# Two gelu layers of an MLP: bank products copied to SBUF, gelu on two tiles at a time

## The reference

```
h = silu(lin(x, w1_w, w1_s)) * lin(x, w2_w, w2_s)
h = gelu(lin(h, h1_w, h1_s), approximate=False)
h = gelu(lin(h, h2_w, h2_s), approximate=False)
return lin(h, w3_w, w3_s)
```

## Time and profile before

| | us |
|---|---|
| median of 3 runs (lowest, highest) | 5497.53 (5493.53, 5498.82) |
| the profiled execution's own time | 5515.07 |
| its span in the trace | 5513.2 |
| granted clock of TensorE, mean over the span | 0.876 |
| PE, DVE, ACT, POOL busy | 4705.2, 3863.6, 3379.4, 3919.7 |
| ACT table loads: L1337, L1343, L1266 | 64, 64, 112 |

### The profile page before, as it was taken

How to read it: one execution, slowest core, us unless ns; L and a number is a source line. 1 busy time by engine, 2 the same in 40 slices (tenths; PEclk the granted TensorE clock), 3 DMA queues, 4 the chain that set the end, 5 groups by cost and what they waited for, 6 DMA issues and landing times. The chain is left out here.

```text
span 5513.2 us, 68556 instructions
## 1 busy us (share of the span) xinstructions
PE 4705.2 (85%) x21152; PEld 1806.6 (33%) x21152; DVE 3863.6 (70%) x4244; ACT 3379.4 (61%) x3966; POOL 3919.7 (71%) x2272
## 2 busy tenths in 40 slices
PE   8649998998999899898989998998999795199991
PEld 4301112223223222222232232222222344188880
DVE  6758888888988898889889888988898502100003
ACT  5646666778776877777777778777777532011111
POOL 0059998998999899899989998998899300411114
PEclk9855558989999999999989999999999896599995
DMA  3357666776777677766767776776677221255542
GB/s 104 107 199 255 239 232 222 266 259 234 247 253 249 224 257 259 251 234 241 265 235 248 259 258 228 256 258 251 233 251 252 101 84 50 102 178 177 178 166 95
DMA packets 313969, 1166.11 MB, mean 212 GB/s; under 512 B 70672, under 2 KB 120336, under 8 KB 303632
## 3 DMA queue, kind: packets, MB, share of 16 engines
q1 hardware_dynamic: 295088, 1058.96, 55.0%
q0 software_dynamic: 18528, 102.77, 5.6%
HBM read 1106.28 MB, written 65.80 MB: 213 GB/s over the span
## 5 line engine op out<-in xcount | busy, mean ns | idle before, releaser
L1609 POOL TENSOR_TENSOR s_h<-s_decay,s_h 128x768 f32<-128x768 f32 x2048 | 3708.0, 1850 | 272.8 <-ACT s_decay L1261 247.2
L1647 DVE TENSOR_TENSOR s_h<-s_h,bank 128x1024 f32<-128x1024 f32 x2048 | 2470.5, 1216 | 389.7 <-POOL s_h L1609 210.6
L1261 ACT ACTIVATE s_decay<-s_decay,s_a_neg 128x1536 f32<-128x1536 f32 x1024 | 1605.8, 1568 | 127.7 <-DMA s_decay<-dt_rows 127.0
L893 PE MATMUL bank<-s_h,s_cdiag 128*32 128x512 f32 x8192 | 1251.7, 687 | 5.8 <-ACT s_y L1273 5.8
L1266 ACT ACTIVATE bank<-bank,s_a_neg 128x512 f32<-128x512 f32 x1024 | 672.7, 657 | 735.5 <-PE bank L881 732.4
L867 PE MATMUL bank<-s_vrow,s_brow 9*128 9x512 bf16 x4096 | 844.8, 422 | 266.6 <-DVE s_h L1647 238.9
L1637 DVE TENSOR_TENSOR s_h<-bank,s_h 128x512 f32<-128x512 f32 x1024 | 699.5, 683 | 0.2
L867 PEld LDWEIGHTS bank<-s_vrow,s_brow 9*128 9x128 bf16 x4096 | 208.6, 92 | 1488.6 <-issue 1485.2
L1005 PE MATMUL bank<-m_mb,m_w 128*128 128x512 f32 x1024 | 524.8, 642 | 0.9 <-ACT m_mb L1339 0.9
L991 PE MATMUL bank<-m_ma,m_w 128*128 128x512 f32 x1024 | 519.2, 636 | 0.0
L881 PE MATMUL bank<-s_drow,s_unit 3*128 3x512 bf16 x1024 | 433.1, 423 | 75.7 <-DMA s_drow<-dt_parts 46.6
(11 more groups left out here) (200 smaller groups left out, 3898.0 us busy)
## 6 DMA issues: line engine op xcount, KB each, us to landing
s_decay<-dt_rows SPq DMA_DIRECT2D x1024, 768.0 KB, 5.4
m_w<-in_units SPq DMA_DIRECT2D x210, 512.0 KB, 5.2
s_vrow<-v_parts SPq DMA_DIRECT2D x1024, 36.0 KB
s_brow<-b_parts SPq DMA_DIRECT2D x1024, 9.0 KB
v_parts<-p_part SPq DMA_DIRECT2D x24, 512.0 KB, 3.0
slots<-in_x_tiles SPq DMA_DIRECT2D x128, 80.0 KB, 4.7
e_xs<-slots SPq DMA_DIRECT2D x39, 256.0 KB
expert_out<-e_made SPq DMA_DIRECT2D x39, 256.0 KB, 5.7
```

Of the source, the lines that this page charges most:

```text
L893: mm = pe.matmul(bank[q * 32:(q + 1) * 32, Y0], cdiag[:, hf * LANES + q, at * BLK:(at + 1) * BLK], h[:, t % 2, hf * LANES + q], start=(at ...
L1261: act.activation(decay[:, k % RING], decay[:, k % RING], ACT.Exp, scale=a_neg[:, 1:2]).then_inc(decay_ok, 1)
L1609: pool.tensor_tensor(h[:, t % 2, g * PAIR:(g + 1) * PAIR, DCOLS:], decay[:, k % RING, g % 2 * PAIR:(g % 2 + 1) * PAIR], h[:, (t + 1) % 2, ...
L1647: dve.tensor_tensor(h[:, t % 2, g * PAIR:(g + 1) * PAIR], h[:, t % 2, g * PAIR:(g + 1) * PAIR], bank[:, X0 + n % 2 * PAIR:X0 + (n % 2 + 1) ...
```

## The change

`gelu_1` and `gelu_2` are split. Each tile's product is now copied out of the bank with its scale by an Identity activation into the place in SBUF where the gelu's result stood. After every second tile the gelu table is loaded and one gelu of 128x1024 is taken in place over both tiles. Two semaphores are new, `h1_cp` and `h2_cp`, which count the copies: they now free the bank (`FREED_BY`, and in the last chunk the waits of `hidden_1` and `hidden_2`). `h1_ok` and `h2_ok` count the gelus, four a layer instead of eight, and the next layer waits for all four. The scale moves from the gelu to the copy, so the same numbers are computed.

```diff
-            "up": ("hid_ok", KH), "h1": ("h1_ok", KH), "h2": ("h2_ok", KH), "out": ("at_add", 2), "w3": ("x2_ok", 2)}
+            "up": ("hid_ok", KH), "h1": ("h1_cp", KH), "h2": ("h2_cp", KH), "out": ("at_add", 2), "w3": ("x2_ok", 2)}
...
                     if tail and j >= 4:
-                        pe.wait_ge(S("h1_ok"), FIRST + m * KH + j - 3)
+                        pe.wait_ge(S("h1_cp"), FIRST + m * KH + j - 3)
...
                     if j == 0:
-                        pe.wait_ge(S("h1_ok"), FIRST + (m + 1) * KH)
+                        pe.wait_ge(S("h1_ok"), FIRST + (m + 1) * (KH // 2))
...
             def gelu_1(m, j, tail):
-                act.preload_act_table_set("gelu_and_others")
                 act.wait_ge(S("h1_ps"), FIRST + m * KH + j + 1)
-                act.activation(mb[:, j], bank[:, j % 4 if tail else M0], ACT.Gelu, scale=k_["sh1"][:, j:j + 1]
-                               ).then_inc(S("h1_ok"), 1)
+                act.activation(mb[:, j], bank[:, j % 4 if tail else M0], ACT.Identity, scale=k_["sh1"][:, j:j + 1]
+                               ).then_inc(S("h1_cp"), 1)
+                if j % 2 == 1:
+                    act.preload_act_table_set("gelu_and_others")
+                    act.wait_ge(S("h1_cp"), FIRST + m * KH + j + 1)
+                    act.activation(mb[:, j - 1:j + 1], mb[:, j - 1:j + 1], ACT.Gelu).then_inc(S("h1_ok"), 1)
```

More of the change, by code:

```diff
@@ L677, in stream_phase @@
         COUNTS = """z_ps z_th z_free z_ok sq rs_ln rs_ok g_ok gT_ps gT_ok o_ps o_add xt_ps xt_ok
-            gate_ps g_th g_free g_ok2 up_ps hid_ok h1_ps h1_ok h2_ps h2_ok w3_ps x2_ok xsq xrs_ln xrs_ok xr_ok
+            gate_ps g_th g_free g_ok2 up_ps hid_ok h1_ps h1_cp h1_ok h2_ps h2_cp h2_ok w3_ps x2_ok xsq xrs_ln xrs_ok xr_ok
             xn_ps xn_ok qk_ps qk_cp qk_sq qk_ln qk_rs qk_n kT_ps ew_ok qT_ps eq_ok v_ps kv_ok seeded cw_ok
@@ L999, in hidden_2 @@
                     if j == 0:
-                        pe.wait_ge(S("h1_ok"), FIRST + (m + 1) * KH)
+                        pe.wait_ge(S("h1_ok"), FIRST + (m + 1) * (KH // 2))
                     if tail and j >= 4:
-                        pe.wait_ge(S("h2_ok"), FIRST + m * KH + j - 3)
+                        pe.wait_ge(S("h2_cp"), FIRST + m * KH + j - 3)
                 slot, _ = place(m, f"h2{j}")
@@ L1013, in mlp_out @@
                     loaded(m, "w3b")
-                    pe.wait_ge(S("h2_ok"), FIRST + (m + 1) * KH)
+                    pe.wait_ge(S("h2_ok"), FIRST + (m + 1) * (KH // 2))
                 t = 2 * pair + i
@@ L1336, in gelu_1 @@
             def gelu_1(m, j, tail):
-                act.preload_act_table_set("gelu_and_others")
                 act.wait_ge(S("h1_ps"), FIRST + m * KH + j + 1)
-                act.activation(mb[:, j], bank[:, j % 4 if tail else M0], ACT.Gelu, scale=k_["sh1"][:, j:j + 1]
-                               ).then_inc(S("h1_ok"), 1)
+                act.activation(mb[:, j], bank[:, j % 4 if tail else M0], ACT.Identity, scale=k_["sh1"][:, j:j + 1]
[4 more added lines that the diff above has]
+                    act.activation(mb[:, j - 1:j + 1], mb[:, j - 1:j + 1], ACT.Gelu).then_inc(S("h1_ok"), 1)
             def gelu_2(m, j, tail):
-                act.preload_act_table_set("gelu_and_others")
                 act.wait_ge(S("h2_ps"), FIRST + m * KH + j + 1)
-                act.activation(ma[:, j], bank[:, j % 4 if tail else M0], ACT.Gelu, scale=k_["sh2"][:, j:j + 1]
-                               ).then_inc(S("h2_ok"), 1)
+                act.activation(ma[:, j], bank[:, j % 4 if tail else M0], ACT.Identity, scale=k_["sh2"][:, j:j + 1]
+                               ).then_inc(S("h2_cp"), 1)
+                if j % 2 == 1:
+                    act.preload_act_table_set("gelu_and_others")
+                    act.wait_ge(S("h2_cp"), FIRST + m * KH + j + 1)
+                    act.activation(ma[:, j - 1:j + 1], ma[:, j - 1:j + 1], ACT.Gelu).then_inc(S("h2_ok"), 1)
             def mean_square_x(m, i):
```

## The result

The changed kernel takes 5603.54 us (median of 4 runs, 5597.68 to 5618.11), against 5498.17 for the one before (4 runs, 5493.53 to 5500.31). The ratio is 1.0186, with a 95% interval of 1.0167 to 1.0205: slower by 105 us, where 68 us were forecast. The direction held. The size was 37 us short and lies outside the forecast band of 40 to 95 us, which had the chance 0.68; the wider range for 8 in 10 (5525 to 5605) holds it by 1.5 us.

A forecast was written before the change was run, and what follows sets the result against it. The stream was taken to last as long as POOL's multiplications plus its waits, nearly all for ACT's exponential. 95 - 32 = 63, plus 5, gave 68 us on 5497.5: 5566; band 5537 to 5592 (0.68), 8 in 10 5525 to 5605.

The forecast's parts named there:

- rival (c): More is lost: DVE cannot recover its delayed multiplication, first tiles gain nothing; 119 + 5 = 124, 5621 us; chance 0.12.
- POOL's work and waits make the stream's length: Streaming phase: POOL's 3708.9 us busy plus waits of 247.2 for ACT and 24.5 for DVE, 3981 of 3990 us.
- First tiles, -32: First tile of each pair, seven chunks: bank's exp begins 1.55 us earlier; POOL gains at most its wait, 32 us.
- Second tiles, +95: Second tile of each pair, seven chunks: the exponential comes up to 2.34 us later, less POOL's slack; 95 us lost.
- about 3.0 at tile 5 of the first layer: Sign to check: POOL's wait at this tile grows from 0.87 to about 3.0 us.
- The load's place: Second tiles: the 1.28 us gelu table load, hidden before in ACT's wait for the product, now stands behind the product.
- Does the delay last? The steps behind are no worse.: Steps behind a gelu: ACT catches up 1.4 us a step, a 4.0 us backlog gone in three; no further loss.
- DVE's multiplication moves by the same amount.: DVE's own multiplication, fed by the bank's exp, moves by the same amount, at the edge just as POOL is.
- The second layer's start stays covered: Second layer starts over 4 us behind the last product; copy, load, gelu take 3.1; uncovered, up to 1 us a chunk.
- The last chunk: After the stream: load and gelu stand behind the copy, 1.28 + 1.06 more at two layers, 4.7 us.
- Rival (a): ACT's accumulated work makes exponentials late: halved switches halve gelu-step waits, -79 / 2 + 5 = -35, 5463 us; chance 0.07.
- Rival (b): POOL's lateness half taken back where DVE or PE were late anyway: 5497 to 5525; 0.05 no change, 0.08 small loss.

The follow-up runs named there:

- e2: Kernel before with only each pair's second tile changed (copy, load, gelu over both tiles), the first as before: 5610.71 us, ratio 1.0192.
- e1: Kernel before with only each pair's first tile changed: copied out of the bank, its gelu left out, the second as before: 5520.57 us, ratio 1.0037.
- e3: Changed kernel with the second tile's gelu table load put ahead of the wait for the product and the copy: 5575.23 us, ratio 1.0136.
- e8: Kernel before with only DVE's two divisions moved, to half-steps 155 and 159: 5510.62 us, ratio 1.0002.
- e10: e4 with DVE's divisions at half-steps 155 and 159, value scan at 97 and 112, silu at 188 and 189: 5482.35 us, ratio 0.9968.
- e4: Changed kernel, but at the second tile: load, first tile's gelu from SBUF, then second's gelu from the bank without copy: 5535.56 us, ratio 1.0067.

## Why the prediction was right, and what it missed

- *The total.* The range held in part by luck: 105 us is outside the 40 to 95 that were thought likely, and 5603.5 is nearer to rival (c)'s 5621 than to 5566.
- *POOL's work and waits make the stream's length.* The sum closes before and after, as it must; that POOL's lateness is one for one where it waits for the exponential is what the tiles show.
- *First tiles, -32.* Measured at their place, -30.7. But that the gain stays was wrong: e2, without it, is not measurably slower than the whole change (1.0192 against 1.0186), and e1, with it alone, is slower than before. The prediction counted the places one by one and subtracted; rival (c)'s half, "the gain at the first tiles does not come", is what the total shows, though not for the reason (c) gave.
- *Second tiles, +95.* Measured +109.9. Tile by tile over the seven chunks, the second layer came within 3 us each: 12.6, 18.6, 15.3, 12.9 against 13.2, 16.0, 14.9, 13.7. The first layer's tiles 5 and 7 are the mis-sized terms: 21.1 and 20.7 against 14.9 and 9.2. They are those where POOL had been made earlier at tile 4 just ahead, and ACT at tile 6: at tile 7 the product now comes 1.05 us behind the exponential, so the whole 2.1 us shows. This is the gain of the first tiles passed on as a loss of the second ones, and e2 confirms it: without that gain the same two tiles cost 15.0 and 9.6 more than before, as forecast. The sign "about 3.0 at tile 5 of the first layer" came out at 3.98 for this reason, while the one for the second layer (4.0) was met. (The reading that the product of the second layer's tile 3 comes 1.97 us behind the exponential in five of seven chunks was wrong; it does so in four, and the sum loses by it well under 1 us.)
- *The load's place.* Right in kind, half right in size: e3 gave 28 us back for 50, as later steps took a part.
- *"Does the delay last? The steps behind are no worse."* This is the step that failed: later steps cost 34.1 us more where I had put nothing. Three places hold most of it: 8.3 us at the step two behind tile 4, the gain of tile 4 passed on (see e2); 7.4 us at three steps behind the value scans, of which four were stretched against two before; and 14.5 us at two steps behind the silu of half-step 180. In the changed kernel that is stretched to 5.9 us in 5 of 6 chunks, before in 2 of 6. As e8's trace has 4 of 6 and 10.5 us more at the same two steps without any change on ACT, how much of the last two belongs to the change is open. DVE, then POOL, in a chunk with the stretched silu:

```profile
2191.50 0.68 DVE L1643 TENSOR_TENSOR s_h<-bank,s_h 128x512 f32<-128x512 f32 x1
2192.10 5.86 DVE L1751 SCALAR_TENSOR_TENSOR m_u<-m_qk,m_u 128x512 f32<-128x512 f32 x1
2197.89 2.34 DVE L1653 TENSOR_TENSOR s_h<-s_h,bank 128x1024 f32<-128x1024 f32 x2
```

```profile
2181.34 16.07 POOL L1615 TENSOR_TENSOR s_h<-s_decay,s_h 128x768 f32<-128x768 f32 x9
2199.17 5.81 POOL L1615 TENSOR_TENSOR s_h<-s_decay,s_h 128x768 f32<-128x768 f32 x3 [1.76 <-DVE s_h L1653]
2208.59 3.60 POOL L1615 TENSOR_TENSOR s_h<-s_decay,s_h 128x768 f32<-128x768 f32 x2 [3.61 <-ACT s_decay L1261]
```

  POOL multiplies on to 2197.41; the silu ends 0.55 us later, and POOL waits 1.76 for the addition behind it. It soon waits 3.61 more, for an exponential that ACT took late because it stood 9.52 us for PE's decay rows. PE in between:

```profile
2199.24 0.61 PE L867 MATMUL bank<-s_vrow,s_brow 9*128 9x512 bf16 x2 [4.63 <-DVE s_h L1653]
...
2202.18 3.77 PE L1005 MATMUL bank<-m_mb,m_w 128*128 128x512 f32 x4
...
2207.53 1.98 PE L1005 MATMUL bank<-m_mb,m_w 128*128 128x512 f32 x4
```

  and the stretch from 2199 to 2205.8 in the view of the earlier trace rows, with the granted clock third from the end:

```profile
2199.00:2205.80 6.80, 6.56 (x16) 1.61 (x16) 6.04 (x7) 0.00 (x0) 5.81 (x3) 0.50 0.46 177
```

  PE had stood idle for DVE 4.63 us; then the clock was granted at half, 1.2 GHz, and four product matmuls took 3.77 us, where they take 1.98 at the full 2.4 GHz a few us later. So TensorE's clock has a part in what a stretched instruction costs. Each of the nine stretched instructions in this trace is followed by two or three waits of POOL and has a stretch at 1.2 GHz at its end. In the one chunk where the clock was low for 3.4 us only, POOL's second wait behind the silu is 2.11 us, in the four others, with 6.8 us, it is 3.37 to 3.61; so some 1.4 of it may be the clock's. Over the stream, from POOL's first multiplication to its last, the clock was low for 940 us, before for 871. No run held the clock, so how much of the 105 us goes through it stays open; the same holds for the 0.3% of e10, whose runs had a mean granted clock of 0.880 against 0.876 for those of the kernel before beside them.
- *"DVE's multiplication moves by the same amount."* DVE waits 62.4 us for the bank's exponential, at 37 places, where it had no such wait: it had slack there before, which is used up. Whether this adds to the length beside POOL's own wait at the same steps no run tells apart.
- *The second layer's start stays covered.* Wrong. PE waits for the gelu at L1005 in 8 cases, 10.1 us in all, 3.24 of it in the last chunk: some 1 us a chunk, the price that I gave for no cover, against one wait of 0.87 before. The last chunk cost 3.7 us, forecast 4.7.
- *Rival (a), ACT's total work counts.* Excluded: e1 takes 153 us off ACT and is slower. *Rival (b)*, half the loss is taken back elsewhere: the reverse happened. *Rival (c)*, more is lost, came nearer in size, with the right half for another reason.

The size that came out, in the two traces, is thus 110 + 34 - 31 - 11 (earlier steps and POOL's own work) + 4 = 106.

## What to carry to other kernels

A table load that lies in a wait cost nothing here; the same load behind the instruction that waits cost its whole length, so the number of loads says little before it is known which of them lie in idle time. Where one engine has hardly any slack, a saving at one place moves every meeting behind it: count the places where two engines collide again with the new timing, and do not add up gains place by place. When work is moved on one engine, look at the durations of the other engines' instructions by shape, not only at their waits; the loss may sit in an instruction that nobody touched, and a table of places tuned for one order need not suit another. Take more than one trace of a kernel before counting rare events in it.

## What the runs showed of the hardware

DVE's division and silu (both tensor operands in SBUF, 128x512) took 0.63 to 0.69 us when POOL had nothing to do. Beside POOL's multiplications they lasted, but for the cases below, to the end of the multiplication that POOL was at, plus 0.55 us: 0.75 to 2.36 us. The value scan (128x520) took 1.22 us alone and ended 1.1 us behind POOL's multiplication: 1.2 to 2.9 us. DVE's multiplication with one operand in the bank keeps its 683 ns in both kernels, whatever POOL does. The Trainium skill (SBUF — State Buffer, Who interferes with whom) says this of the two kinds: two SBUF inputs contend with a GpSimd instruction that reads SBUF, at most one input (outside the modes that use two ports) doesn't, and the lock is exclusive, so that the later one waits for the whole instruction. These rows agree.

What neither I nor that page had: in some cases DVE doesn't get in at the next end of a multiplication of POOL but misses two or three ends in a row, and gets in only when POOL runs dry, after 5.9 to 6.5 us (6.4 to 7.0 for the scan). Over eight kernels (before, after, e1 and e4 to e8), 19 of 96 divisions, 20 of 96 silus and 25 of 96 value scans in the stream did so. By how long ahead of POOL's next start they had started: of the divisions 9 of 12 at 0.0 to 0.2 us and 10 of 29 at 0.5 to 0.6, none of the 55 others; of the silus 20 of 36 at 1.7 to 1.8 us, none of the 60 others; of the scans 16 of 37 at 0.5 to 0.6 and 9 of 24 at 1.7 to 1.8, none of the 35 others. So the moment at which DVE's instruction comes matters, which fits that ten half-steps on DVE are worth 25 us; but it doesn't decide alone: in e4, six divisions started 0.14 to 0.18 us ahead, three took 6.05 to 6.08 us and three 0.75 to 0.77. What decides stays open: no run varied the moment alone.

With the same number of instructions and no edit to DVE's list, the trace of e1 has DVE busy 50 us longer than before; with three tables changed, e10's has it 44 us shorter. The busy time of an engine whose instructions another can hold up is thus not a sum of fixed durations.
